# Layer two's attention: sharing a batch's 16th power by score tiles instead of by columns of every tile, and taking tiles 4 and 5 first

## The reference, cut to what matters

```
cos_sim = clip(Q K^T, -0.999, 0.999)
scores  = 1 - arccos(cos_sim) / pi
W       = power(maximum(scores, 1e-6), 16)
out     = (W / (sum(W) + 1e-6)) V
```

## Time and profile before

| | before |
|---|---|
| median of three runs | 6679.3 us |
| the profiled execution's own time | 6678.16 us |
| its span (first to last instruction) | 6676.4 us |
| busy: ScalarE (ACT) | 6177.6 us (93%) |
| busy: VectorE (DVE) | 5850.0 us (88%) |
| busy: GpSimd (POOL) | 4185.5 us (63%) |
| busy: TensorE matmuls (PE) | 3870.0 us (58%) |

### The profile page before, as it was taken

How to read it: one execution, slowest core, us unless ns; L and a number is a source line. 1 busy time by engine, 2 the same in 40 slices (tenths; PEclk the granted TensorE clock), 3 DMA queues, 4 the chain that set the end, 5 groups by cost and what they waited for, 6 DMA issues and landing times. The chain is left out here.

```text
span 6676.4 us, 49638 instructions
## 1 busy us (share of the span) xinstructions
PE 3870.0 (58%) x17072; PEld 1359.1 (20%) x17072; DVE 5850.0 (88%) x5940; ACT 6177.6 (93%) x1923; POOL 4185.5 (63%) x1127
## 2 busy tenths in 40 slices
PE   5777777777776764544454454444545444454545
PEld 2222222222222420111111121111112111111213
DVE  7867677767767679999999999999999999999996
ACT  3699999999999349999999999999999999999996
POOL 0399999999996006565565656556565656556563
PEclk8899999999998875566656665555656566665657
DMA  4311111111111420000000000000000000000003
GB/s 150 97 27 22 25 27 26 27 27 20 27 25 49 165 86 6 15 8 9 8 14 10 8 15 8 9 8 15 9 8 15 8 9 8 15 9 8 15 6 103
DMA packets 448852, 191.93 MB, mean 29 GB/s; under 512 B 348038, under 2 KB 429849, under 8 KB 446698
## 3 DMA queue, kind: packets, MB, share of 16 engines
q1 hardware_dynamic: 448618, 188.89, 11.1%
HBM read 112.52 MB, written 76.28 MB: 28 GB/s over the span
## 5 line engine op out<-in xcount | busy, mean ns | idle before, releaser
L1322 POOL TENSOR_TENSOR work<-work 128x1776 f32<-128x1776 f32 (+3 forms) x696 | 2149.0, 3088 | 55.3
L1114 PE MATMUL psS<-q_stack,k_stack 96*128 96x512 bf16 x2048 | 1034.0, 607 | 1761.0 <-DVE work L1230 1695.4
L981 POOL TENSOR_TENSOR work<-work 128x4096 f32<-128x4096 f32 x249 | 1737.7, 7013 | 152.6 <-ACT work L886 152.6
L896 DVE TENSOR_SCALAR work<-psS 128x1024 f32<-128x1024 f32 x1024 | 1198.1, 1218 | 555.0 <-PE psS L798 553.6
L1319 POOL TENSOR_SCALAR work<-work 128x1776 f32<-128x1776 f32 (+2 forms) x174 | 290.8, 1671 | 1990.6 <-ACT work L1204 1983.3
L1225 DVE TENSOR_SCALAR work<-psS 128x1024 f32<-128x1024 f32 x1024 | 1205.0, 1218 | 42.2 <-PE psS L1114 18.1
L1230 DVE TENSOR_TENSOR work<-psS,work 128x1024 f32<-128x1024 f32 x1024 | 1200.8, 1214 | 0.0
L1236 DVE SCALAR_TENSOR_TENSOR work<-work 128x2048 f32<-128x2048 f32 x512 | 1139.1, 2283 | 30.2 <-ACT work L1200 30.2
L1196 ACT ACTIVATE work<-work 128x2048 f32<-128x2048 f32 (+2 forms) x259 | 910.7, 3565 | 53.9 <-DVE work L1230 53.8
L1204 ACT ACTIVATE work<-work 128x6144 f32<-128x6144 f32 (+2 forms) x174 | 907.8, 5217 | 32.1 <-DVE work L1236 32.1
L1200 ACT ACTIVATE work<-work 128x2048 f32<-128x2048 f32 (+1 forms) x343 | 916.0, 2741 | 1.0
(11 more groups left out here) (139 smaller groups left out, 3398.0 us busy)
## 6 DMA issues: line engine op xcount, KB each, us to landing
qk_parts<-work SPq DMA_DIRECT2D x64, 384.0 KB, 3.3
q_stack<-qk_parts SPq DMA_DIRECT2D x384, 64.0 KB, 2.3
k_stack<-qk_parts SPq DMA_DIRECT2D x384, 64.0 KB, 2.3
xT_store<-work SPq DMA_DIRECT2D x2, 4096.0 KB, 15.8
v_store<-work SPq DMA_DIRECT2D x16, 512.0 KB, 3.3
v_tile<-v_store SPq DMA_DIRECT2D x64, 128.0 KB, 2.8
ffn_in<-xT_store SPq DMA_DIRECT2D x64, 128.0 KB, 2.7
y_store<-ffn_out SPq DMA_DIRECT2D x64, 128.0 KB, 2.4
```

Source lines behind the costliest of these rows:

```text
L896: nc.vector.tensor_scalar(lane(g)[:, 0, half * 1024:(half + 1) * 1024], m.psS[half][:, :], ZERO_SHIFT, None, ALU.max).then_inc(s_gd, 1)
L981: nc.gpsimd.tensor_tensor(lane(g, 2), lane(g, 2), lane(g, 2), ALU.mult).then_inc(s_wp, 1)
L1114: last = nc.tensor.matmul(m.psS[half][:, q * 512:(q + 1) * 512], m.k_stack[b][0:ROWS, kt * P:(kt + 1) * P], m.q_stack[b][0:ROWS, c:c + 512 ...
L1322: nc.gpsimd.tensor_tensor(part, part, part, ALU.mult).then_inc(s_pp, 1)
```

## The change

The 16th power is no longer cut by columns of every unit but by units of a batch of six: ScalarE takes units 0, 1 and 2 whole and columns 0 to 1631 of unit 3; VectorE takes the rest of unit 3 (416 columns) and columns 1504 to 2047 of unit 4 (544 columns); GpSimd takes unit 5 whole and then columns 0 to 1503 of unit 4. Per batch of six each engine has as many columns as before (7776, 960 and 3552). The batches of 2, 4 and 2 units have tables of their own. From the sigmoid on the units go in the order 4, 5, 0, 1, 2, 3: the sigmoid in parts of 1, 1, 2 and 2 units, the tangents one by one, and the arctan in **three** parts instead of two: units 4 and 5, then 0 to 2, then 3. GpSimd starts on unit 5 after the first arctan. TensorE waits for a unit only on the engines that have a share in that unit.

```diff
-    def pow_cuts(j):
-        return (1296, 1456) if j < NB - 1 else (1600, 1600)
-    def thirds(j):
-        return [(0, sizes[j] // 2), (sizes[j] // 2, sizes[j] // 2)]
-    def tan_parts(j):
-        return {6: [(0, 1), (1, 1), (2, 2), (4, 2)], 4: [(0, 1), (1, 1), (2, 2)], 2: [(0, 1), (1, 1)]}[sizes[j]]
+    def rsin_parts(j):
+        return {6: [(4, 1), (5, 1), (0, 2), (2, 2)], 4: [(3, 1), (0, 1), (1, 2)], 2: [(1, 1), (0, 1)]}[sizes[j]]
+    def angle_parts(j):
+        return {6: [(4, 2), (0, 3), (3, 1)], 4: [(3, 1), (0, 2), (2, 1)], 2: [(1, 1), (0, 1)]}[sizes[j]]
+    def act_powers(j):
+        return {6: [(0, 3, T), (3, 1, 1632)], 4: [(0, 2, T), (2, 1, 1408)], 2: [(0, 1, T), (1, 1, 1200)]}[sizes[j]]
+    def dve_powers(j):
+        return {6: [(4, 1504, T), (3, 1632, T)], 4: [(2, 1408, T)], 2: []}[sizes[j]]
+    def pool_powers(j):
+        return {6: [(5, 0, T), (4, 0, 1504)], 4: [(3, 0, T)], 2: [(1, 1200, T)]}[sizes[j]]
...
-                chunk = 2 * j + p // (sizes[j] // 2) + 1
-                pe.wait_ge(s_w, chunk)
-                if j < NB - 1:
-                    pe.wait_ge(s_pw, 2 * STEPS * j + STEPS + 4 if chunk % 2 else STEPS * chunk)
-                pe.wait_ge(s_pp, STEPS * chunk)
+                for c, (first, n, _) in enumerate(act_powers(j)):
+                    if first <= p < first + n:
+                        pe.wait_ge(s_w, so_far(act_powers, j) + c + 1)
+                for c, (unit, _, _) in enumerate(dve_powers(j)):
+                    if unit == p:
+                        pe.wait_ge(s_pw, STEPS * (so_far(dve_powers, j) + len(dve_powers(j))))
+                for c, (unit, _, _) in enumerate(pool_powers(j)):
+                    if unit == p:
+                        pe.wait_ge(s_pp, STEPS * (so_far(pool_powers, j) + c + 1))
...
-                    for p, size in thirds(i):
-                        act.wait_ge(s_z, starts[i] + p + size)
-                        nc.scalar.activation(cosine(i, p, size), cosine(i, p, size), ACT.Arctan).then_inc(s_at, 1)
+                    for p, size in angle_parts(i):
+                        act.wait_ge(s_z, starts[i] + max(in_order(rsin_parts(i), u) for u in range(p, p + size)))
+                        nc.scalar.activation(cosine(i, p, size), cosine(i, p, size), ACT.Arctan).then_inc(s_at, size)
```

More of the change, by code:

```diff
@@ L1019, in batch_of, with so_far, in_order @@
         return j, g - starts[j]
-    def pow_cuts(j):
-        return (1296, 1456) if j < NB - 1 else (1600, 1600)
-    def thirds(j):
-        return [(0, sizes[j] // 2), (sizes[j] // 2, sizes[j] // 2)]
     def log_parts(j):
         return {6: [(0, 3), (3, 2), (5, 1)], 4: [(0, 2), (2, 1), (3, 1)], 2: [(0, 1), (1, 1)]}[sizes[j]]
-    def tan_parts(j):
-        return {6: [(0, 1), (1, 1), (2, 2), (4, 2)], 4: [(0, 1), (1, 1), (2, 2)], 2: [(0, 1), (1, 1)]}[sizes[j]]
+    def rsin_parts(j):
[8 more added lines that the diff above has]
+        return {6: [(5, 0, T), (4, 0, 1504)], 4: [(3, 0, T)], 2: [(1, 1200, T)]}[sizes[j]]
+    def so_far(parts, j):
+        return sum(len(parts(i)) for i in range(j))
+    def in_order(parts, p):
+        done = 0
+        for first, n in parts:
+            done += n
+            if first <= p < first + n:
+                return done
     last_batch = {n: batch_of(KT * n + KT - 1)[0] for n in range(TILES)}
@@ L1198, in _ @@
                     act.wait_ge(s_ls, starts[i + 1])
-                    for p, size in tan_parts(i):
+                    for p, size in rsin_parts(i):
                         nc.scalar.activation(square(p, size), square(p, size), ACT.Sigmoid, scale=-0.5)\
                             .then_inc(s_rs, size)
-                    for p, size in thirds(i):
-                        act.wait_ge(s_z, starts[i] + p + size)
-                        nc.scalar.activation(cosine(i, p, size), cosine(i, p, size), ACT.Arctan).then_inc(s_at, 1)
+                    for p, size in angle_parts(i):
+                        act.wait_ge(s_z, starts[i] + max(in_order(rsin_parts(i), u) for u in range(p, p + size)))
+                        nc.scalar.activation(cosine(i, p, size), cosine(i, p, size), ACT.Arctan).then_inc(s_at, size)
                     nc.scalar.preload_act_table_set("natural_log_exp_and_others")
-                    for c, (p, size) in enumerate(thirds(i)):
-                        part = cosine(i, p, size)[:, :, 0:pow_cuts(i)[0]]
-                        act.wait_ge(s_at, 2 * i + c + 1)
+                    act.wait_ge(s_at, starts[i + 1])
+                    for p, size, cols in act_powers(i):
+                        part = cosine(i, p, size)[:, :, 0:cols]
                         nc.scalar.activation(part, part, ACT.Ln, bias=0.5, scale=2.0 / PI).then_inc(s_ln, 1)
-                    for c, (p, size) in enumerate(thirds(i)):
-                        part = cosine(i, p, size)[:, :, 0:pow_cuts(i)[0]]
-                        act.wait_ge(s_ln, 2 * i + c + 1)
+                    for c, (p, size, cols) in enumerate(act_powers(i)):
+                        part = cosine(i, p, size)[:, :, 0:cols]
+                        act.wait_ge(s_ln, so_far(act_powers, i) + c + 1)
                         nc.scalar.activation(part, part, ACT.Exp, scale=16.0).then_inc(s_w, 1)
@@ L1233, in tangents @@
             def tangents(j):
[L1234 to L1237, removed]
+                for first, n in rsin_parts(j):
+                    dve.wait_ge(s_rs, starts[j] + in_order(rsin_parts(j), first))
+                    for p in range(first, first + n):
+                        nc.vector.scalar_tensor_tensor(cosine(j, p), square(p), RSIN_MAX, cosine(j, p),
+                                                       ALU.min, ALU.mult).then_inc(s_z, 1)
                 dve.wait_ge(s_z, starts[j + 1])
             def powers(j):
[L1241 to L1247, removed]
+                parts = [cosine(j, p)[:, 0, a:b] for p, a, b in dve_powers(j)]
+                base = STEPS * so_far(dve_powers, j)
+                for c, (p, _, _) in enumerate(dve_powers(j)):
+                    dve.wait_ge(s_at, starts[j] + in_order(angle_parts(j), p))
+                    nc.vector.tensor_scalar(parts[c], parts[c], 2.0 / PI, 0.5, ALU.mult, ALU.add).then_inc(s_pw, 1)
+                for i in range(len(parts), STEPS * len(parts)):
+                    part = parts[i % len(parts)]
+                    dve.wait_ge(s_pw, base + i - len(parts) + 1)
+                    nc.vector.tensor_tensor(part, part, part, ALU.mult).then_inc(s_pw, 1)
             def head_out(n):
@@ L1314, in _ @@
             for j in range(NB):
[L1315 to L1318, removed]
+                for c, (p, first, last) in enumerate(pool_powers(j)):
+                    part = cosine(j, p)[:, 0, first:last]
+                    chunk = so_far(pool_powers, j) + c
+                    pool.wait_ge(s_at, starts[j] + in_order(angle_parts(j), p))
                     nc.gpsimd.tensor_scalar(part, part, 2.0 / PI, 0.5, ALU.mult, ALU.add).then_inc(s_pp, 1)
```

## The result

The changed kernel takes 6798.03 us (median of 4 runs, 6796.52 to 6799.44) against 6678.49 us, a ratio of 1.0178 with a 95% interval of 1.0166 to 1.019: 119.5 us **slower**. The forecast was 11.3 us faster, and the range ended at 6684. It is wrong by sign and size. The profiled execution took 6797.01 us, with a span of 6795.2.

The account below looks back on a forecast made before the run. VectorE and ScalarE were both taken as full, the slower loop setting each batch; plain 3.5 plus after-ReLU 6.8 plus ends 1.0 made 11.3 us less, 6668 us against 6679.3, 8-in-10 range 6654 to 6684.

Parts of the forecast that it names:

- the wait before the last arctan: ScalarE's third arctan no longer waits for the last tangent: loop shorter by 0.24 us (plain) or 0.40 us (after ReLU).
- the slow rival: GpSimd's early start makes VectorE's last tangent after a ReLU batch wait 1.93 us: about 6726 us, chance 13%.
- Columns cost nothing: Power step: same columns per engine, VectorE's eight squarings still 4.62 us, so no term.
- A third arctan at 0.10 us: ScalarE: one more arctan instruction per batch costs about 0.10 us, alone 8 us over 83 batches.
- No gain beyond ScalarE's lateness: VectorE's loop is untouched, so a batch gains at most ScalarE's lateness: 10.3 us in sum.
- the term for the 20 batches after a ReLU batch: Those where ScalarE is late by 0.43 us gain 0.34 us each, 6.8 us in all.
- GpSimd waits for the last tangent, at no cost: GpSimd starts 1.70 us sooner but waits for VectorE's last tangent; its chain ends as late as before, cost nothing.
- GpSimd first: GpSimd takes the shared way into SBUF before VectorE's last tangent after a ReLU batch: about 6726 us, chance 13%.
- all of the wait comes back: VectorE's loop has unseen slack, so the whole 25.3 us are won: 6653 us, chance 12%.
- TensorE and the ends: TensorE's matmuls start some 4 us sooner for no gain; first and last batches together gain 1.0 us.
- The tie in the batch of four: GpSimd's start and VectorE's third tangent at about the same time; if GpSimd wins, some 2.3 us reach the end.
- The gain of 1.0 us at the ends: Last batches: fewer GpSimd columns and an earlier first arctan gain 1.0 us, ends -1.9 and +2.3.

Follow-up runs that it names:

- the run with two: The changed kernel with two arctan instructions in a batch of six, units 4 and 5, then 0 to 3: 6790.14 us, ratio 1.0168.
- fifth-tangent run: The changed kernel with the arctan of units 0 to 2 waiting for the fifth tangent instead of the sixth: 6664.85 us, ratio 0.9979 to the kernel before.
- the last run: The changed kernel with the fifth-tangent wait, sigmoids one by one up to unit 1, and 1712 instead of 1632 columns of unit 3 for ScalarE: 6647.65 us.

## Why the prediction was wrong

- **The step that failed** is in "the wait before the last arctan": "the second the fifth". It was the table of parts read as if waits were per tangent. The second arctan waits for the sixth tangent, so the last wait did not vanish but moved forward by one instruction and grew from 0.25 to 2.01 us, with four units of arctan behind it instead of three. It is a misreading of the code, not of the profile: the diff has the `max(in_order(...))`, and the sentence under it says that `in_order` counts to the end of the part that holds a unit. None of the rivals had it; the slow rival (6726 us) had the right sign for another reason.
- **The rest of that step was right.** With the wait on the fifth tangent ScalarE's idle time before arctans is 0.0 us. In that trace plain batches last 47.92 us (forecast 47.94), 19 of the batches after a ReLU batch 47.84 (47.9), ReLU batches 49.0 to 49.4 (49.0 to 49.3). Of the 11 others nine gained 0.15 us (48.12 instead of 48.27) that I had not seen.
- **Columns cost nothing**: nearly right. VectorE's multiply-adds got cheaper.
- **A third arctan at 0.10 us**: right, 0.095 us by the run with two.
- **No gain beyond ScalarE's lateness**: right as a rule, and the term for the 20 batches after a ReLU batch was mis-sized. With the arctan cut in the kernel before, 18 of them gained all of their 0.43 us where 0.34 was taken; the two others gained 0.09, as their distance before was 2.12 to 2.13 us and not 2.48. The 83 batches gained 12.4 us where the sum was 10.3, out of the 25.3 us of waiting that the group showed. That the whole program gained 10.5 us, within 0.2 of the sum, is partly chance.
- **GpSimd waits for the last tangent, at no cost**: right, 3.59 us and 0.1 us of time. So "GpSimd first" falls, and so does "all of the wait comes back": holding GpSimd back changes nothing, and the gain stayed at about half of the wait. One thing in that passage was misread: the row of 3.30 us stands there for an instruction with two inputs, but it is a multiply-add and has one. The squaring behind it, with two, took 3.47 us beside GpSimd where 0.65 is usual.
- **TensorE and the ends**: its sums do start earlier (around 4800 us, 0.9 to 1.1 us before the sigmoids' table load in the fifth-tangent run, 3.3 to 3.9 us after it before), and VectorE waits less than 1 us for scores. The tie in the batch of four went to VectorE. The gain of 1.0 us at the ends doesn't show: from the end of the 83 batches to the end of the span it is 160.4 us in the fifth-tangent run and 160.2 in the kernel before.

## What to carry to other kernels

When parts of unequal size pass through several engines, write each wait as the number of finished pieces in the producer's own order, and check the values: a wait rounded up to the end of a part did no harm where parts end together, and cost 133 us here where they did not. In a loop over two full engines count what lies **behind the last hand-over**, since that is what the consumer's loop is made of; idle time before an instruction is worth only what the other engine's loop leaves room for (10 to 12 of 25 us here). Then look at the first hand-over, from the sigmoids to the tangents, as well: here it gave 21.9 us, twice as much as the last one.

## What the runs showed of the hardware

**A waiting GpSimd did not get in between VectorE's instructions.** In the batch of four of the fifth-tangent run VectorE does four tangents back to back. GpSimd's multiply-add starts at 6558.00, while the second runs; the third and the fourth are this row:

```profile
6558.10 4.48 DVE L1260 SCALAR_TENSOR_TENSOR work<-work 128x2048 f32<-128x2048 f32 x2
```

```profile
6558.00 6.33 POOL L1345 TENSOR_SCALAR work<-work 128x2048 f32<-128x2048 f32 x1 [8.09 <-ACT work L1227]
```

It lasts 6.33 us, 4.43 more than the 1.90 of an unhindered one: it waited for the third and the fourth tangent. The changed kernel shows it again with one tangent fewer. There GpSimd starts inside the third tangent, 0.43 us ahead of the fourth, and waits for that too:

```profile
6691.20 2.28 DVE L1257 SCALAR_TENSOR_TENSOR work<-work 128x2048 f32<-128x2048 f32 x1
```

```profile
6690.77 4.47 POOL L1342 TENSOR_SCALAR work<-work 128x2048 f32<-128x2048 f32 x1 [9.96 <-ACT work L1224]
```

The Trainium skill, "SBUF — State Buffer", section "Who interferes with whom", gives the shared way to whoever issues first. That holds for the last tangent of a batch of six. Here a GpSimd instruction that was already held up lost to a tangent that started after it. That the third tangent won in the first case says less: the extra time is 0.15 us shorter than the overlap both here (4.43 of 4.58) and in a batch of six (1.69 of 1.84), so GpSimd seems to need the way only some 0.15 us after its recorded start (an estimate from these rows), and its lead was 0.10. The other way round VectorE did get in between GpSimd's instructions: in the kernel before a multiply-add and two squarings, from 6553.37 on the earlier trace rows, took 3.30, 3.47 and 3.59 us, and each ended 0.35 to 0.51 us after one GpSimd squaring had ended.

**Multiply-adds over three segments are dearer on VectorE.** Two of 3 x 160 columns took 0.88 us together where GpSimd was idle; the two of 544 and 416 contiguous columns take 0.72 us (this pair starts where GpSimd is idle, in the fifth-tangent run), with the same 960 columns:

```profile
4519.12 0.72 DVE L1269 TENSOR_SCALAR work<-work 128x544 f32<-128x544 f32 x2
```

The gaps between the segments alone don't explain it: one of 2 x 160 columns took 0.33 us in the kernel before (at 6589.16), and contiguous ones of 336 take 0.32 in the last run. One of 3 x 160 takes 0.48. Whether the odd number of segments does it was not tried. The squarings of the same columns take 4.62 us either way.
